# Selective scan start-up: GpSimd makes two of the eight input rests, and the last softplus is spread over later units

## The reference

```python
# 4096 tokens (2 sequences of 2048), d = 256 channels, n = 16 states
A = -exp(log_A)                                   # (d, n)
dt = softplus(u @ W_dt.T + b_dt + dt_bias)        # (tokens, d)
Bt = (u @ W_B.T + b_B).reshape(b, l, d, n)
Ct = (u @ W_C.T + b_C).reshape(b, l, d, n)
A_bar = exp(dt[..., None] * A)
B_bar = (A_bar - 1.0) / A * Bt
x_in = B_bar * u[..., None]
h_t = A_bar_t * h_{t-1} + x_in_t                  # for each channel and state
y_t = sum_n(Ct_t * h_t) + D_skip * u_t
```

## Time and the profile before

| what | value |
|---|---|
| median of 3 runs | 2807.53 us (2797.03 to 2808.0) |
| profiled execution, its own time | 2793.68 us |
| its span, first to last instruction | 2792.0 us |
| mean granted TensorE clock | 0.965 |
| TensorE matmuls busy | 2558.3 us (92%) |
| VectorE busy | 1957.6 us (70%) |
| ScalarE busy | 1388.3 us (50%) |
| GpSimd busy | 1103.5 us (40%) |
| scan, first to last matmul | 1738.90 to 2474.29 us of the span |

### The profile page before, as it was taken

One profiled execution on the slowest core, in us unless ns is written; L12 is line 12 of the kernel. 1 busy time (PEld: TensorE's weight loads), 2 busy tenths in 40 slices (PEclk: granted clock), 3 DMA queues, 4 the chain that ended last, 5 costly groups with the idle time before them and its releaser, 6 DMA issues. The chain is left out here.

```text
span 2792.0 us, 43868 instructions
## 1 busy us (share of the span) xinstructions
PE 2558.3 (92%) x15059; PEld 1581.8 (57%) x15059; DVE 1957.6 (70%) x4039; ACT 1388.3 (50%) x2469; POOL 1103.5 (40%) x1090
## 2 busy tenths in 40 slices
PE   8999999999999999989999998899999999976983
PEld 4433333333333333347777776688888888854762
DVE  3766666667666766345666654999999999975246
ACT  2455555555555555643455443655555555543320
POOL 3522222222222221110011000699898998854444
PEclk9999999999999999999999998999999999987997
DMA  8633332232223220110000000000000000023775
GB/s 240 169 59 64 59 61 58 45 70 56 55 55 55 55 55 28 63 51 16 23 24 16 16 8 20 12 11 11 11 11 11 11 11 11 8 82 121 245 229 176
DMA packets 109601, 166.41 MB, mean 60 GB/s; under 512 B 15876, under 2 KB 74296, under 8 KB 106232
## 3 DMA queue, kind: packets, MB, share of 16 engines
q1 hardware_dynamic: 99064, 143.24, 20.4%
q0 software_dynamic: 6144, 16.79, 1.9%
q10 hardware_dynamic: 4224, 4.19, 0.4%
HBM read 97.66 MB, written 62.01 MB: 57 GB/s over the span
## 5 line engine op out<-in xcount | busy, mean ns | idle before, releaser
L646 ACT ACTIVATE ssm_in_dt<-att_s 128x512 f32<-128x512 f32 (+3 forms) x1280 | 616.0, 535 | 457.5 <-PE att_s L543 231.3
L735 DVE TENSOR_REDUCE att_partmax<-att_s 128x1 f32<-128x512 f32 x768 | 492.3, 685 | 261.3 <-PE att_s L529 217.4
L517 PE MATMUL att_s<-att_ks,att_qs 49*128 49x512 f32 (+3 forms) x1280 | 491.3, 442 | 46.9 <-DVE att_partmax L735 39.5
L543 PE MATMUL att_s<-att_qs,att_ks 49*128 49x512 f32 (+3 forms) x1280 | 466.3, 430 | 9.0 <-ACT ssm_in_dt L646 6.8
L1789 POOL TENSOR_TENSOR ssm_cc<-ssm_cc,ssm_h 128x512 f32<-128x512 f32 x256 | 332.2, 1298 | 244.7 <-DVE ssm_h L1846 244.0
L543 PEld LDWEIGHTS att_s<-att_qs,att_ks 49*128 49x128 f32 x1280 | 214.0, 186 | 373.5 <-ACT ssm_in_dt L646 270.8
L434 POOL TENSOR_SCALAR_AFFINE_SELECT ssm_in_dt<-ssm_in_dt 128x256 f32<-128x256 f32 x256 | 104.0, 406 | 783.7 <-ACT ssm_in_dt L646 756.3
L586 PE MATMUL att_o_ps<-ssm_in_dt,att_vst 128*32 128x512 f32 (+3 forms) x2560 | 347.9, 552 | 3.6 <-ACT ssm_in_dt L646 3.4
L1804 POOL TENSOR_TENSOR ssm_out_z<-ssm_out_z,ssm_cc 128x512 f32<-128x512 f32 x256 | 336.8, 1316 | 0.1
L1729 ACT ACTIVATE ssm_cc<-ssm_c_ps,ssm_cur 128x512 f32<-128x512 f32 x256 | 199.2, 778 | 225.4 <-PE ssm_c_ps L1678 225.4
L517 PEld LDWEIGHTS att_s<-att_ks,att_qs 49*128 49x128 f32 x1280 | 213.5, 186 | 124.8 <-DVE att_partmax L735 99.4
(11 more groups left out here) (323 smaller groups left out, 4193.7 us busy)
## 6 DMA issues: line engine op xcount, KB each, us to landing
qk_halves<-ssm_in_dt SPq DMA_DIRECT2D x64, 256.0 KB
moe_sorted<-att_hidden SPq DMA_DIRECT2D x31, 512.0 KB, 9.2
moe_rows<-moe_sorted SPq DMA_DIRECT2D x62, 256.0 KB
moe_answers<-moe_mixed SPq DMA_DIRECT2D x62, 256.0 KB
att_far<-bias_tables SPq DMA_DIRECT2D x96, 136.0 KB, 8.3
att_stage_q<-qk_halves SPq DMA_DIRECT2D x96, 128.0 KB, 4.4
att_stage_k<-qk_halves SPq DMA_DIRECT2D x96, 128.0 KB, 6.0
ssm_raw<-in_w_bc SPq DMA_DIRECT2D x30, 256.0 KB, 2.6
```

The costliest lines, as they stand in the source:

```text
L517: mm = nc.tensor.matmul(s1[:, S1_BANK[at], 0:hi - lo], qs[p % 3][half(b, ROWS), I * P:(I + 1) * P], ks[p % 3][half(b, ROWS), lo:hi], start ...
L543: mm = nc.tensor.matmul(s2[:, turn % RING, 0:hi - lo], ks[p % 3][half(b, ROWS), J * P:(J + 1) * P], qs[p % 3][half(b, ROWS), lo:hi], start ...
L646: nc.scalar.activation(prob[:, b, step % 2, x * CH + lo:(x + 1) * CH], s2[:, turn % RING, 0:CH - lo], ACT.Exp, scale=1.0 / HD).then_inc(s2 ...
L735: nc.vector.tensor_reduce(most, piece, AX, ALU.max).then_inc(s1_read, 1)
```

## The change

GpSimd gets, at the head of its list, the rests of chunks 1 and 2, with a semaphore of their own; VectorE's `round_lo(1)` and `round_lo(2)` go. TensorE waits for the semaphore that belongs to the chunk. On ScalarE `round_hi(1)` moves ahead of the exp of the last softplus, and the logarithm moves from unit 2 to unit 3. On VectorE the first two instructions of `correction` move from unit 0 to unit 1 and the second of them now releases the logarithm; the third instruction (`larger`, the maximum) moves to unit 4, and `softplus` from unit 3 to unit 5.

```diff
+        BY_POOL = (1, 2)
+        def rounded(eng, ch):
+            if ch in BY_POOL:
+                eng.wait_ge(pool_lo_ready, BY_POOL.index(ch) + 1)
+            else:
+                eng.wait_ge(lo_ready, len([c for c in range(ch + 1) if c not in BY_POOL]))
@@ tensor
-                            eng.wait_ge(lo_ready, ch + 1)
+                            rounded(eng, ch)
@@ scalar
-                    if first and i == 2:
+                    if first and i == 3:
                         eng.wait_ge(last_corr, 1)
                         nc.scalar.activation(t.last_expn, t.last_expn, ACT.Ln, bias=one[:]).then_inc(last_log, 1)
...
+            round_hi(1)
             eng.wait_ge(last_abs, 1)
             nc.scalar.activation(t.last_expn, t.last_expn, ACT.Exp).then_inc(last_expn, 1)
-            round_hi(1)
@@ gpsimd
+            for ch in BY_POOL:
+                eng.wait_ge(hi_ready, ch + 1)
+                nc.gpsimd.tensor_tensor(lo[:, :, chunk(ch)], u[:, ch], hi[:, :, chunk(ch)].bitcast(F32),
+                                        ALU.subtract).then_inc(pool_lo_ready, 1)
             multiply(0, 0)
@@ vector
-                    if first and i == 0:
+                    if first and i == 1:
                         correction()
-                    if first and i == 3:
+                    if first and i == 4:
+                        larger()
+                    if first and i == 5:
                         softplus()
...
-                step(nc.vector.tensor_tensor(corr, expn, corr, ALU.subtract))
-                nc.vector.scalar_tensor_tensor(out=corr, in0=pre, scalar=0.0, in1=corr, op0=ALU.max, op1=ALU.add).then_inc(last_corr, 1)
+                nc.vector.tensor_tensor(corr, expn, corr, ALU.subtract).then_inc(last_corr, 1)
+            def larger():
+                eng.wait_ge(last_corr, 1)
+                step.go(nc.vector.scalar_tensor_tensor(out=t.last_corr, in0=t.last_pre, scalar=0.0, in1=t.last_corr, op0=ALU.max, op1=ALU.add))
             def softplus():
+                step.wait()
                 eng.wait_ge(last_log, 1)
...
-            round_lo(1)
             eng.wait_ge(cur_ready, 1)
             driven(0, 0)
-            round_lo(2)
             driven(0, 1)
```

More of the change, by code:

```diff
@@ L1646, in phase_scan @@
         raw_loaded = [sp.sem(f"raw_loaded{m}") for m in range(KT)]
-        hi_ready, lo_ready = sp.sem("hi_ready"), sp.sem("lo_ready")
+        hi_ready, lo_ready, pool_lo_ready = sp.sem("hi_ready"), sp.sem("lo_ready"), sp.sem("pool_lo_ready")
         par_ready, skip_ready = sp.sem("par_ready"), sp.sem("skip_ready")
```

## The result

| | before | changed |
|---|---|---|
| median of 20 runs | 2796.61 us (2788.14 to 2808.0) | 2790.47 us (2780.9 to 2800.53) |
| profiled execution, its own time | 2793.68 us | 2790.79 us |
| span | 2792.0 us | 2789.1 us |

The ratio is 0.9973 with a 95% interval of 0.9961 to 0.9985, so the change saves 0.27% (0.15 to 0.39%), some 7.5 us with 4 to 11 possible; the two medians differ by 6.1 us. In the profiles the scan alone is 4.85 us shorter, 0.17%, which lies in both intervals.

What follows compares the result with a forecast made beforehand. TensorE paces the steady scan, and late VectorE rests delay its start-up; an earlier start ends the scan earlier. Late rest 2 absorbed, start-up -4.6, steady part 0: 2807.53 - 4.6 = 2802.9 us, range 2790 to 2811.

Steps and rivals of the forecast that it cites:

- walk of the prediction: Scan start-up, queues followed instruction by instruction: scan(1) at 1752.45 instead of 1756.78 us, unit 7 3.9 us earlier.
- the wait for unit 9's C buffer: Entry into the gapless stretch: unit 9's C half could start at 1778.4 but waits 0.3 us for outward(7).
- the signs of being wrong: GpSimd rest over 3.3 us, TensorE waiting for a C buffer in units 9 to 12, or start-up clock under 0.75.
- the late rest 2: GpSimd's rest of chunk 2 in the start-up: makes unit 2 1.2 us late, 2.1 if it takes 3.27 us.
- the sum: Whole scan: late rest of chunk 2 +1.2 us, absorbed because unit 3 waits for lo(3); start-up -4.6; steady part 0.
- the two open cases: Unit 7's clock: at 2.4 GHz the gain is 5.2 us, slow as before 3.9; about equally open.
- The 4.6: Start-up gain in us, taken as the middle between unit 7 at full clock and unit 7 slow as before.
- the prediction's own 1.1 us: A VectorE instruction with two SBUF inputs ends 1.1 us behind the GpSimd instruction that it meets.
- carried to the median: Last step, from the profiled execution to the three runs' median: 2807.53 - 4.6 = 2802.9 us.
- Softplus giving most back: Rival: the later softplus and further blocked VectorE instructions leave a gain of 1 to 3.5 us, 2804.0 to 2806.5; chance 0.24.
- Nothing moves: Rival: GpSimd's slow elementwise work and low clock in two more units leave the time within 1 us, 2807.5; chance 0.10.
- The low clock from unit 5 to 8: Rival: TensorE stays at 1.2 GHz in these units, up to 2.7 us slower, 2810.2; chance 0.06.

Runs made afterwards that it cites:

- rests 4 and 6: The changed kernel with GpSimd also making the rests of chunks 4 and 6, chunk 2 rounded early, correction in unit 2, logarithm in unit 5; 0.9961 of the kernel before.

## Why the prediction was right and wrong

**The mechanism and its sizes held.** Measured from unit 0's first matmul (1738.90 before, 1739.73 after):

| | walk of the prediction | measured |
|---|---|---|
| unit 2 | 9.8 | 9.83 |
| scan(1) | 13.55 | 13.53 |
| unit 4 | 17.4 | 17.44 |
| unit 5 | 23.9 | 24.09 |
| unit 7 | 32.5 | 32.79 |
| unit 8 | 35.3 | 35.68 |

GpSimd's rest took 2.38 (2.39 taken), hid the first time and made unit 2 late the second; the small parameter instruction lasted 2.30 instead of 0.18 (some 2.3 of waiting allowed for); the wait for unit 9's C buffer was 0.3, as worked out, though the prediction also lists such a wait among the signs of being wrong. The scan gained 4.85 us against 4.6.

That the late rest 2 was absorbed, the run with chunk 2 rounded early shows. The reason in the sum, that unit 3 waits for lo(3) and not for unit 2, is wrong, and the walk itself has it otherwise (lo(3) at 1751.25, unit 2 at 1751.5). In the trace lo(3) ended at 1752.08 and unit 3 started at 1752.45, straight behind unit 2; what took up the delay was the wait ahead of unit 4.

**The clock.** Unit 7 ran at full clock, 2.89 us instead of 4.44, so 1.55 of the 5.14 us of the start-up are clock and 3.59 its earlier start. Of the two open cases the faster one (5.2) came. The 4.6 was the middle of the two and no case of its own; that 4.85 lies so near it is in part luck. The 0.35 that it lacks to 5.2 are small steps of the walk: unit 5 was already 0.2 late, VectorE's period from one rest's end to the next was 4.36 and 4.34 us instead of 4.30 (ends at 1763.69, 1768.05 and 1772.39), and unit 7 took 2.89, not 2.80.

Unit 5, after 3.58 us of idling, ran at the low level and took 5.28 us. The walk had left this open and not charged it, and unit 6 started at 29.37 instead of 28.2. It cost nothing in the end, as three queues show (ScalarE's outward(5) and its rounding of chunk 7, GpSimd's multiply, VectorE's lo(7)):

```profile
1769.34 0.78 ACT L1738 ACTIVATE ssm_cc<-ssm_c_ps,ssm_cur 128x512 f32<-128x512 f32 x1 [3.08 <-PE ssm_c_ps L1687]
1770.02 1.04 ACT L1723 CAST ssm_hi<-ssm_in_u 128x1024 fp32r<-128x1024 f32 x1
...
1769.99 1.29 POOL L1798 TENSOR_TENSOR ssm_cc<-ssm_cc,ssm_h 128x512 f32<-128x512 f32 x1 [0.80 <-DVE ssm_h L1859]
...
1771.16 1.23 DVE L1836 TENSOR_TENSOR ssm_lo<-ssm_in_u,ssm_hi 128x1024 fp32r<-128x1024 f32 x1 [0.74 <-ACT ssm_hi L1723]
```

The late C of unit 5 kept back the rounding of chunk 7, so lo(7) started late but ran unheld and ended at 1772.39. Started in time, at about 1770.4, it would have met the multiply, which ended at 1771.28, and by the prediction's own 1.1 us it would have ended at about the same 1772.4.

**The step that failed is the last one, "carried to the median".** I took 2807.53, the median of three runs, as the base. Twenty runs put the kernel before at 2796.61; two of the three are the slowest of the twenty. So the 2802.9, meant as a gain, lies above even the unchanged kernel. It was wrong by 12.4 us, 10.9 of it from the base; the other 1.5 are the medians' fall of 6.1 us against 4.6. The profiled execution's own 2793.68 turned out nearer: less 4.6 it gives 2789.1, within 1.4 us of the measured 2790.47, which is luck as well, since it is one execution, 2.9 us below the twenty's median. I had both numbers and wrote that the trace couldn't explain the 13.9 us between them; the centre belonged between the two, not at the upper. Even the median of the four executions at hand, 2802.28, would have given 2797.7, 7 us too much. Why two of the first three took so long is not shown; no profile shows them.

**The size of the timed gain**, 0.27% and 0.22% in two sets, stands above my 0.16%, but both intervals hold it (their low ends are 0.15 and 0.09%). In microseconds, 7.5 by the ratio and 6.1 by the medians lie above the forecast's 3.5 to 6, and the profiles' 4.85 within it. What the profiles show is 0.17%; whether the rest is scatter or a gain outside the scan stays open.

**The rivals.** Softplus giving most back: it did cost its 0.3 and no more. Nothing moves: excluded by both intervals. The low clock from unit 5 to 8: one unit was slow.

## What to carry to other kernels

Where a fast engine waits at a start-up, walk the queue of the engine that feeds it instruction by instruction; what frees the feeder is worth what stands in front of the next hand-over, not how long the moved work takes on its new engine. Before giving work to GpSimd, look at which VectorE instructions with two SBUF inputs, or `tensor_scalar` with input and output in SBUF, it will meet: the same rest on GpSimd gave 0.4 us when the correction met it, and 4.3 with a second rest moved, chunk 2 rounded early and the correction placed elsewhere. And take the base of an absolute forecast from all executions at hand, the profiled one among them: for a change of 0.2% the base is the larger error.

## What the runs showed of the hardware

**Scatter ahead of the scan and the chip behind it.** In ten profiled executions, whose code ahead of the scan is the same, the scan's first matmul comes between 1734.88 and 1752.68 us. The stretches up to it, changed kernel run again and rests 4 and 6:

```profile
0.00:1739.41 1739.41, 1619.33 (x10860) 832.81 (x10861) 1103.98 (x2716) 903.39 (x1725) 329.05 (x448) 0.98 0.25 57
```

```profile
0.00:1752.68 1752.68, 1635.00 (x10861) 836.31 (x10861) 1104.32 (x2716) 903.06 (x1725) 329.22 (x448) 0.97 0.24 57
```

VectorE, ScalarE and GpSimd did the same work to 0.4 us, TensorE was busy 15.7 us longer at a granted clock of 0.97 instead of 0.98. Over the ten, TensorE's busy time up to that point goes from 1615.19 us (scan from 1734.88) to 1635.00 (scan from 1752.68). The timed runs agree: of the twenty of the changed kernel the fastest, 2780.9 us, has a mean granted clock of 0.967 and the slowest, 2800.53, one of 0.959. So a good part of the 20 us between a kernel's runs goes with how the clock is granted, much of it in the phases ahead, and the changed stretch must be read from its own borders. The last phase, from its first transfer to the end, took 309.7 and 310.8 us in the profiles of the first result and 276.1 to 281.1 in the eight experiments, at 192 and 191 GB/s against 211 to 215. Why the same transfers went faster there is not shown.

**A wait that looks like a long instruction.** 2.30 us for 32 elements, where the same instruction before took 0.18: the profile books the time under GpSimd's rest as busy. It was a `tensor_scalar` with one input and its output in SBUF. The Trainium skill (SBUF — State Buffer, section "Who interferes with whom") names that operation among those that can take the pair of ports which VectorE and GpSimd share; that this one was held to the end of GpSimd's rest agrees. VectorE's 95% busy of the steady scan may hold such time as well, which is not shown: in the kernel before, the rest of the weights (L1819) shows 1.59 to 1.72 us there and 0.68 in unit 0, when GpSimd was idle.
